# A four-stage network on one core: packs of K on GpSimd's queue, sums' inverses without DRAM, a table of laps for the end

## The reference

```
L0  non-local block:  y = softmax(theta(x)^T phi(x)) g(x), phi and g max-pooled 2x2 (256 keys)
                      x1 = BN(W y) + x                       # 64 inner channels
L1  wavelet block:    Haar halves, 1x1 fusion, BN, ReLU, spatial gate (7x7 over mean and max),
                      channel gate, 1x1 projection, BN, ReLU, inverse Haar, + x1      -> x2
L2  attention:        h = GroupNorm16(x2); softmax(q^T k / sqrt(128)) over 1024 keys, one head of
                      128 channels; x3 = proj(...) + x2
L3  transformer:      xn = GroupNorm32(x3); 8 heads of 16 channels, softmax over 1024 keys;
                      x4 = w_out(...) + x3; out = x4 + MLP(GroupNorm32(x4)), hidden 32, GELU
```

## Time and profile before

| | |
|---|---|
| median of 3 runs | 1929.61 us |
| the profiled execution, its span | 1934.16 us, 1932.4 us |
| TensorE busy, mean granted clock | 1639.0 us (85%), 0.847 |
| VectorE, ScalarE, GpSimd busy | 1066.5, 817.6, 221.9 us |
| SyncE's DMA queue | 60.94 MB, 14.6% of the DMA engines' time |
| GpSimd's DMA queue | 0.53 MB, 0.3% |
| chain of waits, shares of the span | TensorE 47%, issue 27%, VectorE 9%, SyncE's queue 7%, ScalarE 5%, DMA 4% |

### The profile page before, as it was taken

One profiled execution on the slowest core, in us unless ns is written; L12 is line 12 of the kernel. 1 busy time (PEld: TensorE's weight loads), 2 busy tenths in 40 slices (PEclk: granted clock), 3 DMA queues, 4 the chain that ended last, 5 costly groups with the idle time before them and its releaser, 6 DMA issues.

```text
span 1932.4 us, 20834 instructions
## 1 busy us (share of the span) xinstructions
PE 1639.0 (85%) x6481; PEld 739.5 (38%) x6481; DVE 1066.5 (55%) x1904; ACT 817.6 (42%) x1514; POOL 221.9 (11%) x201
## 2 busy tenths in 40 slices
PE   6678869989799997999799998999799869876893
PEld 3335525433443344433453344334443334322220
DVE  4334465747367654757377645757376736475301
ACT  1112202556236542656146632655246624652650
POOL 5003102100220003100220003000210021000000
PEclk6778857999789888989799888989889888886855
DMA  2000012011210312020200312030210221202001
GB/s 48 22 22 6 17 33 46 11 39 28 59 20 1 77 23 50 6 63 16 61 20 2 77 32 43 6 77 2 58 20 9 58 48 20 59 17 47 23 1 34
DMA packets 33875, 62.90 MB, mean 33 GB/s; under 512 B 15958, under 2 KB 18142, under 8 KB 33760
## 3 DMA queue, kind: packets, MB, share of 16 engines
q1 hardware_dynamic: 32672, 60.94, 14.6%
q0 software_dynamic: 1088, 0.53, 0.3%
HBM read 18.56 MB, written 4.53 MB: 12 GB/s over the span
## 4 chain that ended last, share of the span: by engine, by line
PE 47%; issue 27%; DVE 9%; SPq 7%; ACT 5%; DMA 4%; POOL 2%; DVEq 0%; POOLq 0%; ACTq 0%
PE ps L1256 46%; DVE mx L1202 4%; DMA kp<-k3l 3%; SPq L632 3%; ACT p L935 2%; SPq L606 2%; DVE x L1151 1%; SPq L654 1%; POOL x L739 1%; DVE x L1156 1%; DVE mv L1054 1%; POOL mv L732 0%; DMA invw<-inverse_sums 0%; SPq L614 0%; DVE mx L1198 0%
## 5 line engine op out<-in xcount | busy, mean ns | idle before, releaser
L1202 DVE TENSOR_REDUCE mx<-ps 128x1 f32<-128x512 f32 x1024 | 645.3, 684 | 275.2 <-PE ps L1256 274.8
L935 ACT ACTIVATE p<-ps 128x512 f32<-128x512 f32 x1024 | 552.7, 600 | 352.7 <-PE ps L1256 350.9
L1256 PE MATMUL ps<-kp,qp 63*128 63x512 f32 x1024 | 430.8, 523 | 127.9 <-DMA kp<-k3l 87.6
L1256 PE MATMUL ps<-qp,kp 64*128 64x512 f32 x1024 | 403.3, 496 | 25.2 <-ACT p L935 20.4
L1256 PEld LDWEIGHTS ps<-qp,kp 64*128 64x128 f32 x1024 | 175.3, 203 | 364.9 <-ACT p L935 227.4
L1256 PE MATMUL ps<-p,vt 128*32 128x512 f32 x2048 | 305.2, 671 | 4.9 <-ACT p L935 4.2
L1256 PEld LDWEIGHTS ps<-kp,qp 63*128 63x128 f32 x1024 | 184.9, 208 | 249.7 <-DVE mx L1202 123.3
L900 ACT ACTIVATE p<-ps 128x512 f32<-128x512 f32 x128 | 76.4, 597 | 230.9 <-PE ps L1256 226.9
L1256 PE MATMUL ps<-p,vT 128*128 128x512 f32 x256 | 149.2, 678 | 0.1
L771 POOL TENSOR_TENSOR acc<-acc,p 128x512 f32<-128x512 f32 x96 | 126.5, 1317 | 172.2 <-ACT p L900 172.2
L1198 DVE TENSOR_REDUCE mx<-ps 128x1 f32<-128x512 f32 x128 | 85.9, 689 | 52.3 <-PE ps L1256 52.0
(11 more groups left out here) (189 smaller groups left out, 1490.1 us busy)
## 6 DMA issues: line engine op xcount, KB each, us to landing
qp<-q3h SPq DMA_DIRECT2D x128, 64.0 KB, 2.4
kp<-k3h SPq DMA_DIRECT2D x128, 64.0 KB, 2.5
xin<-in_x SPq DMA_DIRECT2D x8, 512.0 KB, 5.2
x<-inverse_sums SPq DMA_DIRECT2D x8, 512.0 KB, 3.7
acc<-inverse_sums SPq DMA_DIRECT2D x16, 256.0 KB, 3.5
qp<-q3l SPq DMA_DIRECT2D x64, 64.0 KB, 2.4
kp<-k3l SPq DMA_DIRECT2D x64, 64.0 KB, 2.5
x3a<-x SPq DMA_DIRECT2D x8, 512.0 KB, 3.8
```

The costliest lines, as they stand in the source:

```text
L935: a.activation(p3[:, s % 2, i, :], ps[:, SB + (u + 1) % 3, :], ACT.Exp).then_inc(sem("p3_ready"), 1)
L1202: v.tensor_reduce(mx3[:, i, c, h:h + 1], ps[:, bank, :], AX.X, ALU.max).then_inc(sem("mx3_ready"), 1)
L1256: return nc.tensor.matmul(o, l, r, start=start, stop=stop)
```

## The change

Five things are changed.

1. The K part of `pack` for group 0 leaves SyncE and is issued by GpSimd (12 DMAs an image, from lap `packed_k` on), with semaphores of its own; a small product on GpSimd carries the wait. Q's DMAs and group 1's K stay on SyncE. TensorE waits for Q's and K's semaphores.
2. L0's inverses: two products of `ones` with 512 columns of `x1` give the sums on all partitions, and two reciprocals of 128x512 write them into `x1`. The two DMAs through DRAM are gone.
3. L2's sums (`den2`): the same weights, but 128 columns of `ones` instead of one; the reciprocal reads every 128th.
4. A third table, `LAST`, holds for windows 7 and 8. In it `beside` adds, in window 7, a product of ones in the other 64 rows beside the score tiles (28 in group 0, all 64 in group 1), into banks nobody reads.
5. All tables are chosen anew. In the steady plan: laps 180 instead of 164 (heads stay at 18 and 86), group 1's by-query tiles at laps 8 to 68 (5 to 63 before), L2's at 62 to 86 (56 to 76), group 0's at 92 to 156 (92 to 151), the pack of head 0 ahead of the tail's DMAs.

```diff
 STEADY = {
-    "laps": 164,
+    "laps": 180,
-    "packed": (2, 86),
+    "packed": (0, 86),
+    "packed_k": 86,
...
-            "TL": {0: 74, 2: 78, 5: 82, 7: 84, 9: 88, 11: 89, 13: 91},
+            "TL": {0: 78, 2: 82, 5: 88, 7: 89, 9: 91, 11: 94, 13: 95},
...
-            "L0": {5: 107, 7: 110, 9: 113, 11: 118, 13: 122, 15: 126, 28: 147, 32: 155, 34: 156},
+            "L0": {5: 111, 7: 114, 9: 117, 11: 119, 13: 122, 15: 126, 28: 152, 30: 155, 32: 157, 34: 158},
...
         "Pool": {
-            "TL": {8: 84},
-            "L0": {26: 144},
-            "HN": {4: 5},
+            "TL": {8: 89},
+            "L0": {26: 148},
+            "HN": {4: 8},
         "SP": {
-            "HN": {0: 0, 2: 1, 3: 2},
+            "HN": {0: 1, 2: 3, 3: 4},
...
+LAST = {
...
+    "beside": 73,
...
     def window(bt):
-        at.plan = STEADY_PLAN
+        at.plan = LAST_PLAN if bt.is_last() else STEADY_PLAN
...
# SyncE
-                for dst, parts in ((qp[:, hd // 2, :], (q3h, q3l, q3h)), (kp[:, hd // 2, :], (k3h, k3h, k3l))):
-                    for n, part3 in enumerate(parts):
-                        sp.dma_start(raw(dst[r + HD * n:r + HD * (n + 1), :]), raw(part3[c:c + HD, :])).then_inc(sem(f"packed{i // 2}"), 16)
+                for n, part3 in enumerate((q3h, q3l, q3h)):
+                    sp.dma_start(raw(qp[r + HD * n:r + HD * (n + 1), hd // 2, :]), raw(part3[c:c + HD, :])).then_inc(sem(f"packed_q{i // 2}"), 16)
+                if g:
+                    for n, part3 in enumerate((k3h, k3h, k3l)):
+                        sp.dma_start(raw(kp[r + HD * n:r + HD * (n + 1), hd // 2, :]), raw(part3[c:c + HD, :])).then_inc(sem(f"packed_k{i // 2}"), 16)
# GpSimd
+            def carry_wait(bt, g):
+                wait(pool_e, sem("waits_carried"), bt, 1, 0)
+                nc.gpsimd.tensor_tensor(idle[:, 1:2], neg_half[:, 0:1], neg_half[:, 0:1], ALU.mult).then_inc(sem("waits_carried"), 1)
+            def pack(bt, g, i):
+                hd = GH * g + i
+                r, c = SPAN * (hd % 2), HD * hd
+                if i == 0:
+                    wait(pool_e, sem("vt3_ready"), bt, NG, g + 1)
...
+                    carry_wait(bt, g)
+                for n, part3 in enumerate((k3h, k3h, k3l)):
+                    nc.gpsimd.dma_start(raw(kp[r + HD * n:r + HD * (n + 1), hd // 2, :]), raw(part3[c:c + HD, :])).then_inc(sem(f"packed_early_k{i // 2}"), 16)
             def passes(bt, plan, sides):
                 for p in range(plan.laps):
+                    if (bt + 1).exists() and p in range(plan.packed_k, plan.packed_k + 3 * GH, 3):
+                        pack(bt + 1, 0, (p - plan.packed_k) // 3)
# VectorE
-                yield at(bt, "L0", 28)
-                wait(dve, sem("den0_ps"), bt)
-                v.reciprocal(inv0[:], ps[:, bank_of(bt), 0:NC]).then_inc(sem("inv0_ready"), 1)
+                for h in range(NH):
+                    yield at(bt, "L0", 28 + 2 * h)
+                    wait(dve, sem("den0_ps"), bt, NH, h + 1)
+                    v.reciprocal(half(x1, h), ps[:, bank_of(bt), :]).then_inc(sem("inv0_ready"), 1)
# TensorE
+            def beside(i, bank):
+                rows = slice(SPAN * (1 - i % 2), SPAN * (2 - i % 2))
+                mm(ps[:, bank, :], ones_r[rows, :], ones_r[rows, :].unsqueeze(1).to_broadcast([SPAN, 4, 128]))
...
-                for c in range(NC):
-                    last = mm(ps[:, bank_of(bt), c:c + 1], x1[:, c::NC], ones[:, 0:1])
-                last.then_inc(sem("den0_ps"), 1)
+                for h in range(NH):
+                    yield at(bt, "L0", 27 + 2 * h)
+                    if h:
+                        wait(pe, sem("inv0_ready"), bt, NH, h)
+                    else:
+                        wait(pe, sem("p0_added"), bt)
+                    mm(ps[:, bank_of(bt), :], ones[:], half(x1, h)).then_inc(sem("den0_ps"), 1)
...
-                        wait(pe, sem("inv0_ready"), bt)
+                        wait(pe, sem("inv0_ready"), bt, NH)
...
-                    last = mm(ps[:, VB, c:c + 1], acc[:, h, c::NC // 2], ones[:, 0:1])
+                    last = mm(ps[:, VB, 128 * c:128 * (c + 1)], acc[:, h, c::NC // 2], ones[:])
...
-                        wait(pe, sem(f"packed{i // 2}"), mb, 16 * 12 * NG, 16 * 12 * (mg + 1))
+                        wait(pe, sem(f"packed_q{i // 2}"), mb, 16 * 6 * NG, 16 * 6 * (mg + 1))
+                        wait(pe, sem(f"packed_k{i // 2}" if mg else f"packed_early_k{i // 2}"), mb, 16 * 6)
...
+                            if plan.beside and not attention and (g or p < plan.beside and i % 2 == 0):
...
+                                beside(i, MB + i % 2 if g else XB)
```

More of the change, by code:

```diff
@@ L57 @@
-    "turned": {"DVE": (67, 150, 218), "PE": (71, 151, 218), "ACT": (72, 152, 218), "SP": (73, 152, 218)},
-    "moved": (58, 221),
[1 row of a table removed]
+    "laps": 225,
+    "scores2": (79, 80, 82, 84, 86, 88, 90, 92, 93, 95, 99, 101, 103, 105, 107, 109),
+    "values2": (81, 83, 85, 87, 89, 91, 94, 94, 100, 102, 104, 104, 106, 108, 110, 112),
+    "copy2": (94, 113),
+    "den2": (98, 114),
+    "inv2": (99, 116),
+    "spread2": (103, 118),
+    "out2": (105, 120),
+    "base2": 32,
+    "rec2": (99, 116),
+    "vt": (0, 153),
@@ L60 @@
+    "turned": {"DVE": (70, 158, 221), "PE": (75, 160, 221), "ACT": (76, 160, 221), "SP": (77, 160, 221)},
+    "moved": (58, 224),
[1 row of a table added]
     "at": {
@@ L118 @@
 STEADY = {
-    "laps": 164,
+    "laps": 180,
+    "scores2": (0, 1, 2, 3, 4, 5, 6, 7, 8, 9, 10, 11, 12, 13, 14, 15),
+    "values2": (1, 2, 3, 4, 5, 6, 7, 8, 11, 11, 12, 12, 13, 14, 15, 16),
+    "copy2": (8, 18),
+    "den2": (9, 17),
+    "inv2": (10, 18),
+    "spread2": (12, 20),
+    "out2": (16, 29),
+    "base2": 0,
+    "rec2": (9, 19),
+    "vt": (0, 86),
+    "packed": (0, 86),
+    "packed_k": 86,
+    "tiles": ("000000002222211500102111111111011100111111111111102111121111110011111000000000000000000000000000000000000000000000000000000000000000000000000000000000000000000000000000000000000000",
+              "000000000000000000000000000000000000000000000000000000000000001010000110111102120100011000000000000000000000000000000000000000000000000000000000000000000000000000000000000000000000",
+              "000000000000000000000000000000000000000000000000000000000000000000000000000000000000000000001031111111011111111111111111111111111112101111111111110110211111100000000000000000000000"),
+    "turned": {"DVE": (69, 87, 157), "PE": (71, 87, 157), "ACT": (71, 89, 158), "SP": (72, 90, 158)},
+    "moved": (82, 110),
[8 rows of a table added]
+        },
+        "DVE": {
[6 rows of a table added]
+        },
+        "ACT": {
[6 rows of a table added]
+        },
+        "Pool": {
+            "L1": {0: 0},
+            "Q2": {4: 15},
+            "Q3": {4: 47},
+            "TL": {8: 89},
+            "L0": {26: 148},
+            "HN": {4: 8},
+        },
+        "SP": {
+            "L1": {0: 0},
+            "Q2": {0: 0},
+            "Q3": {0: 0},
+            "TL": {15: 98},
+            "L0": {0: 98, 18: 132},
+            "HN": {0: 1, 2: 3, 3: 4},
+        },
+    },
+    "fill": "000000000000000000000000000000000000000000000000000000000000000000000000000000000000000000000000000000000000000000000000000000000000000000000000000000000000000000000000000000000000",
+}
+LAST = {
+    "laps": 180,
     "scores2": (0, 1, 2, 3, 4, 5, 6, 7, 8, 9, 10, 11, 12, 13, 14, 15),
@@ L162 @@
             "L1": {0: 0},
-            "Q2": {4: 14},
-            "Q3": {4: 48},
-            "TL": {8: 84},
-            "L0": {26: 144},
-            "HN": {4: 5},
+            "Q2": {4: 15},
+            "Q3": {4: 47},
+            "TL": {8: 89},
+            "L0": {26: 148},
+            "HN": {4: 8},
         },
@@ L196, in __call__ @@
     def __call__(self, bt, stage, k):
-        name = stage if self.plan is STEADY_PLAN else f"{stage}.{bt.b + bt.off}"
+        name = f"{stage}.{bt.b + bt.off}" if self.plan is FIRST_PLAN else stage
         return self.plan.at[self.engine].get(name, {}).get(k, 0)
@@ L211, in is_first, with is_last @@
         return isinstance(self.b, int) and self.b == -1
+    def is_last(self):
+        return isinstance(self.b, int) and self.b >= B - 1
     def is_number(self, n):
@@ L340, in __init__ @@
         self.base2, self.rec2, self.out2 = table["base2"], table["rec2"], table["out2"]
+        self.beside = table.get("beside", 0)
         self.fill = [int(n) for n in table.get("fill", "0" * self.laps)]
-        self.packed, self.vt, self.moved = table["packed"], table["vt"], table["moved"]
+        self.packed, self.packed_k, self.vt, self.moved = table["packed"], table["packed_k"], table["vt"], table["moved"]
         self.maxima = [maxima2_order(tiles) if group is None else maxima_order(tiles) for tiles, group in zip(table["tiles"], groups)]
```

90 lines of the change are left out of this document (39 added, 51 removed), and 103 rows, old and new, of tables (FIRST, LAST, STEADY).

## The result

The changed kernel takes 1866.32 us in the median (1865.36 to 1871.38, 4 runs), the kernel before 1931.81 beside it (1924.23 to 1935.13). The ratio is 0.9672, 95% interval 0.9636 to 0.9707: 65.5 us, 3.3%, faster. The forecast was 1865. The sum came out, its terms only in part: one was 15 us off, and one of up to 21 us the other way was missing. Most of what follows is about those two and about how the others were checked.

A forecast was written before the change was run, and what follows sets the result against it. Bound: TensorE's work divided by its granted clock, plus its waits. Terms -32 -14 -11 -6 +12 +22 +0 -14 -22 = -65 from 1934 give about 1869, against the median 1865 us; own range 1840 to 1893, 8-in-10 range 1825 to 1922.

The forecast's parts named there:

- Gap in windows 1 to 6: TensorE's wait for first packed rows shrinks: -32, half clock behind it -14 (windows 1 to 5); window 6 -11.
- Window 7: Start of window 7, no attention to fill it: SyncE's shorter queue and earlier landing take 6 of 25.3 us.
- GpSimd's `rstd` behind K's packs: Tail's `rstd` stands behind six pack issues on GpSimd; VectorE and TensorE wait 2 us in windows 1 to 6: +12.
- Inverses of the first attention: End of windows 0 to 4: serial chain of wide products and reciprocals is longer, +4.5 us each: +22.
- `den2` with 128 columns: Second attention's sums: wider products hide behind their weight loads, 0 us (bounds 0 and +2.3 a batch).
- Ones: Window 7, group 1 of heads: ones beside score products hold full clock, 16 steps from 4.07 to about 2.7 us: -22.
- Tables: Second attention's maxima reach lap 86, covering the tail's half-clock stretch: 2 us in each of seven windows, -14.
- First plan: First pair's packs on two queues -3.5, batch 0's longer inverse chain +3.5: about 0.
- the moved gap: Rival: window start is tied to VectorE's wavelet sums or attention's exps and GpSimd's adds; 57 us return, 1922; chance 0.14.
- the rival's 3.0 us: Rival: GpSimd's pack issues at lap 86 stretch from 0.81 to 3.0 us beside VectorE, giving 1949; chance 0.08.
- ones-are-useless rival: Rival: ones in window 7's last group don't lift the clock, the 22 us stay, 1887; chance 0.10.
- The clock stays up: Rival: without gap and one-column products most half-clock stretches go, 5 us more in each of seven windows, 1830; chance 0.15.

The follow-up runs named there:

- the later lap: GpSimd's product of gathered heads by inverses (ogc by invw) moved from lap 8 to 18 in the changed kernel: 1844.96 us.
- the best kernel here: Changed kernel with GpSimd's product at lap 18, old first-attention inverses, last windows' den, ogc and inverses behind group 1's packs, group 0's K packs on SyncE: 1822.49 us.

## Why the prediction was right, point by point

- **Gap in windows 1 to 6: forecast -32 - 14 - 11 = -57.** The queue's order undone costs 52, with the maxima's later start left in. Mechanism and size hold: SyncE's order, and slices at half clock behind the gap.
- **Window 7: forecast -6.** The wait is 6.9 us shorter.
- **GpSimd's `rstd` behind K's packs: forecast +12.** The queue does cost, 8 us, but the step is wrong: `rstd` waits for its input and not for the issues, except in window 6 (1.4 us). Right in sign by luck.
- **Inverses of the first attention: forecast +22.** 19 when undone. The reciprocal takes 3.356 us; forecast 3.36 from the earlier trace rows. The place is not as forecast. From TensorE's sum to the next attention the forecast had 21.0 us for 16.8; measured, window by window, it is 16.9, 16.3, 19.5, 19.6 and 17.0, before 16.4, 16.6, 19.0, 19.3 and 16.8, and from GpSimd's sum on 1.1 to 1.8 us more. The new chain runs nearly in the old one's time, in a kernel whose other parts changed as well, and only against the old chain in the same tables does it cost 19. So the total holds, and the sum over the window's end that gave it does not.
- **`den2` with 128 columns: forecast 0.** It is worth 15, a gain. This step failed: it priced the matmuls by their duration and took the clock to be none of their business. The earlier trace rows had the hint, half clock from the narrow sums of `den0` on.
- **Ones: forecast -22.** 21 when taken out; a step is 1.40 us shorter than before, 22 us for the 16 of the forecast.
- **Tables: forecast -14.** Not measured alone. The 54 us of the kernel before with the new table are 52 + 7 of the gap and window 7, less the pile-up, plus what the tables give. With a pile-up of 21 that leaves 16 for the tables, with half of it about 5, with none a loss of 5. Whether the term holds stays open.
- **First plan: forecast about 0.** GpSimd's sum of the first attention in window 0 starts 8.7 us earlier (475.1 us, before 483.7). With the old first plan and the new steady table it is 0.6. With old inverses, narrow `den2` or K on SyncE it stays at 469 to 473, so it is the new table `FIRST` that is worth the 8, which the prediction did not price. The reason it gave, two queues for the first pair, fails: TensorE waits 7.1 us for that pair, and 5.6 with one queue.
- **Missing: `invw` behind head 1's packs: up to +21.** The text said "VectorE's wavelet pile stays" and gave the moved gap a rival through GpSimd's adds, but never followed the DMA that was moved back to the engine that waits for it. With head 1's six issues in front, GpSimd's wait went from 4 to 6 us to 10 to 12. The 21 are what the later lap gives back, and by the waits for the maxima about half of that is new.

The measured terms, with the pile-up at 21, add up to -52 - 7 + 8 + 19 - 15 - 21 + 21 = -47, and with the first plan (8) and the tables (16) to -71, against -65.5. Undoing a part from another start is not exact to better than this. What the prediction missed, gains of 15 and 8 us and a loss of up to 21, largely cancelled, so that 1865 met 1866 is in part luck. Of its rivals, the moved gap was partly true: the pile-up is what it described, at a third of its price or less. GpSimd's issues stayed far under the rival's 3.0 us: 0.48 us in the median, 0.97 at most. The Trainium skill (SBUF — State Buffer, A bandwidth-pool intuition that's wrong) has 3.1 us for such a DMA overlapped with a VectorE copy and puts it down to a port that VectorE holds. The trace agrees in kind, not in size: one issue a window is stretched, by 0.5 us, and it ends just after VectorE's 0.81 us product. The ones-are-useless rival is refuted. "The clock stays up" (1830) did not come. With the change's two new waits taken out, the pile-up and the reciprocals, the kernel is at 1822 to 1831; that it is then the rival come true is argued, not shown.

## What to carry to other kernels

When a DMA moves back in a queue, go to the engine that waits for it, in order, and list what is queued behind that wait; here a product that nothing needed for 70 laps held up six adds that TensorE needed at once. Price a matmul not only by its duration but by what the granted clock does behind it; here narrow ones in a busy stretch cost more than wide ones. A second issuing queue did not pay here: look first whether anything waits for the first queue's issues. And undo each part of a change once: the best kernel here (1822, 2.3% under the changed one) keeps its order, its ones and its wide sums, and drops two of its parts.

## What the runs showed of the hardware

- **Narrow matmuls lower the clock.** In the same place, with the same weight loads, eight 128x1 products go with 0.76, 0.50 and 0.89 of full clock in three slices, eight 128x128 ones with 1.00 in each (window 3; over all sixteen groups 0.73 and 0.89). TensorE's recorded busy time is 4.00 of 4.00 us in either. It cost 15 us in all. The Trainium skill (TensorE: Matmul & The Clock Gate, What's actually happening) says that activity releases the throttle. Recorded busy time does not tell these two cases apart, and the clock does; the measurement decides.
- **A reciprocal costs 4.9 products.** 128x512 out of PSUM: 3356 ns, the product with 1.0 of the same shape 686. The Trainium skill (VectorE: DVE Perf Modes, First, the fixed hardware budget) says that the reciprocal is an iterative divide with a repeat count of 8 in the same pipe. By a factor of eight it would be an estimated 5.5 us; measured is less.
- **Sums of two SBUF operands on VectorE beside GpSimd's adds**: 0.42 us alone, 1.46 us beside a block of them, for 128x256; 0.69 and 1.75 for 128x512. GpSimd's adds slow down too, but less: five in the block take 1.45 us each, 1.28 alone. The larger delay falls on the engine that TensorE waits for.
- **With a second queue the packs land later**: 2.4 (Q) and 2.5 us (K) with SyncE alone, 2.9 (Q, SyncE) and 4.1 (K, GpSimd) with two, 64 KB each.
- **An issue on GpSimd beside VectorE's product of 128x1024 in SBUF** takes up to 0.97 us, 0.48 in the median.
